# One core, a non-local block and two scans: the last stage in pieces, part of it summed ahead, six places for weighed states, diagonals by ScalarE

## The reference, cut to what matters

```python
attention = theta_x @ phi_x / n                    # theta_x, phi_x, g_x: 1x1 convolutions of x
out = conv1x1((attention @ g_x), w_rec, b_rec) * inv + (bn_beta - bn_mean * inv) + x

def _mamba(u, ...):                                # u: 224 sequences of 56 tokens, 256 features
    x, z = split(u @ in_w.T)                       # 512 and 512
    x = silu(conv_b + sum(xpad[:, k:k + L] * conv_w[:, k] for k in range(4)))
    dt_raw, Bm, Cm = split(x @ xp_w.T)             # 16, 16, 16
    dt = softplus(dt_raw @ dt_w.T + dt_b)
    h = exp(dt * A) * h + (dt * x) * Bm            # a scan over the 56 tokens, 512 x 16 states
    y = (sum over states of h * Cm) + x * D
    return (y * silu(z)) @ out_w.T
out = cat_conv_w @ concat([y1, y2]) + cat_conv_b + x
```

## Time and profile before

| | us |
|---|---|
| median of 3 runs | 5613.23 (5611.07 to 5613.51) |
| the profiled execution's own time | 5617.14 |
| its span, first to last instruction | 5615.2 |

### The profile page before, as it was taken

How to read it: one execution, slowest core, us unless ns; L and a number is a source line. 1 busy time by engine, 2 the same in 40 slices (tenths; PEclk the granted TensorE clock), 3 DMA queues, 4 the chain that set the end, 5 groups by cost and what they waited for, 6 DMA issues and landing times. The chain is left out here.

```text
span 5615.2 us, 71207 instructions
## 1 busy us (share of the span) xinstructions
PE 4836.0 (86%) x26046; PEld 3541.9 (63%) x26046; DVE 5064.4 (90%) x3469; ACT 3547.9 (63%) x5534; POOL 5064.0 (90%) x2582
## 2 busy tenths in 40 slices
PE   8888888888888888888788888889989898888887
PEld 7746566656666565656556656666666666666664
DVE  4469999999999999999999999999999999999992
ACT  0067676766666676767566767666666666766662
POOL 0079999999999999999999999999999999999992
PEclk9989999999999999999899999999999999999999
DMA  4232323232232323232323232333232424242423
GB/s 153 102 109 67 116 67 112 77 102 91 89 108 71 116 67 116 67 112 78 111 67 116 67 112 81 109 104 114 93 125 87 134 80 138 77 144 75 140 70 127
DMA packets 242753, 560.65 MB, mean 100 GB/s; under 512 B 29314, under 2 KB 116226, under 8 KB 241252
## 3 DMA queue, kind: packets, MB, share of 16 engines
q1 hardware_dynamic: 230804, 528.00, 29.2%
q10 hardware_dynamic: 11600, 28.10, 1.3%
HBM read 497.86 MB, written 58.15 MB: 99 GB/s over the span
## 5 line engine op out<-in xcount | busy, mean ns | idle before, releaser
L1058 POOL TENSOR_TENSOR dbx<-dtx,b_all 128x896 f32<-128x896 f32 x1792 | 3701.3, 2102 | 0.1
L986 DVE TENSOR_TENSOR_SCAN mamba_ps<-mamba_ps,dbx 128x896 f32<-128x896 f32 x1232 | 2481.8, 2014 | 106.4 <-ACT mamba_ps L860 63.5
L805 PE MATMUL mamba_ps<-ident,hc 128*112 128x128 f32 x14336 | 1867.5, 282 | 167.0 <-POOL hc L1065 135.9
L805 PEld LDWEIGHTS mamba_ps<-ident,hc 128*112 128x112 f32 x14336 | 1668.7, 138 | 507.4 <-issue 255.3
L860 ACT ACTIVATE mamba_ps<-dt,w 128x448 f32<-128x448 f32 x1792 | 1067.7, 629 | 727.3 <-DVE hc L993 580.8
L993 DVE TENSOR_TENSOR hc<-mamba_ps,c_all 128x896 f32<-128x896 f32 x1232 | 1341.7, 1089 | 137.8 <-DVE mamba_ps L986 3.9
L860 ACT ACTIVATE mamba_ps<-dt,a_next 128x448 f32<-128x448 f32 x1792 | 1067.4, 629 | 626.4 <-DVE hc L993 500.9
L1065 POOL TENSOR_TENSOR hc<-hc,c_all 128x896 f32<-128x896 f32 x560 | 1176.0, 2100 | 130.8 <-DVE hc L986 130.4
L986 DVE TENSOR_TENSOR_SCAN hc<-mamba_ps,dbx 128x896 f32<-128x896 f32 x560 | 1129.1, 2016 | 51.0 <-ACT mamba_ps L860 50.9
L702 PE MATMUL mamba_ps<-u,w 128*128 128x448 f32 x1792 | 799.6, 584 | 203.8 <-ACT sz L883 109.3
L713 PE MATMUL mamba_ps<-x,taps 128*128 128x448 f32 (+3 forms) x1792 | 727.0, 550 | 117.2 <-ACT x L874 108.3
(11 more groups left out here) (107 smaller groups left out, 3105.9 us busy)
## 6 DMA issues: line engine op xcount, KB each, us to landing
b_all<-bc_scratch SPq DMA_DIRECT2D x448, 448.0 KB, 5.5
c_all<-bc_scratch SPq DMA_DIRECT2D x448, 448.0 KB, 4.8
u<-u_scratch SPq DMA_DIRECT2D x56, 448.0 KB, 3.3
y_scratch<-ytok SPq DMA_DIRECT2D x56, 448.0 KB, 3.3
src<-y_scratch SPq DMA_DIRECT2D x80, 224.0 KB, 4.5
u_scratch<-ub ACTq DMA_DIRECT2D x28, 448.0 KB, 4.6
xb<-in_x ACTq DMA_DIRECT2D x3, 3136.0 KB, 10.7
src<-in_x SPq DMA_DIRECT2D x40, 224.0 KB, 5.2
```

The lines of the kernel that those rows point to most:

```text
L805: ins = nc.tensor.matmul(y_ps[j % 2][:, c * 128:(c + 1) * 128], hc[g][:, e * T + c * TCH:e * T + (c + 1) * TCH], ident[:, :], start=False, ...
L986: nc.vector.tensor_tensor_scan(dst, h, dbx[n % BX_RING][:, :], 0.0, ALU.mult, ALU.add).then_inc(scan_done, 1)
L1058: nc.gpsimd.tensor_tensor(view(dbx[n % BX_RING], 0, [[T, 2], [1, T]]), view(dtx, j * T, [[0, 2], [1, T]]), view(b_all, 2 * g * T, [[T, 2], ...
```

## The change

- **Schedule.** All slots of the items are new; fa and fb become one item pair f0, f1 of 448 columns, at TensorE's slot 26 and ScalarE's 26 and 29. Three gates move.
- **Pieces and partial sums.** Tiles 29 to 35 get f0 and f1 too: for batch 3 they sum the first model's two blocks and the map's two (eight matmuls of 448), with the bias, and store that to `part_dram`. Tiles 36 to 55 make the full pieces as before.
- **`finish`.** For batch 3 only the second model's two blocks remain (four matmuls per piece); VectorE adds the stored part, loaded over ScalarE's queue. The last piece of batch 2 is made whole between pieces 4 and 5.
- **Places and lags.** `hc` has six places by `n % 6`; `by_pool` keeps ten slots of 32, but with 27 where 30 was; `POOL_LAG` is 5.
- **Diagonals.** At the change ScalarE makes `taps` and `skip`. The convolution waits for its own four diagonals only.
- **Prologue.** The normalisation's chain is cut into steps, one behind each of the pairs 1 to 13 of batch 0.

```diff
 SCHEDULE = {
-    "z0": (0, 0), "x0": (0, 0), "x1": (0, 2), "z1": (0, 3), "z2": (2, 4), "z3": (2, 5), "c0": (4, 5), "c1": (6, 8),
-    "y3": (7, None), "x2": (9, 10), "x3": (10, 11), "c2": (11, 12), "c3": (12, 13), "y0": (13, None), "out0": (15, 17), "xp": (16, 19),
-    "out1": (18, 20), "dt0": (19, 22), "dt1": (19, 22), "fa0": (21, 23), "dt2": (21, 23), "dt3": (22, 24), "fa1": (23, 26), "y1": (24, None),
-    "y2": (31, None), "fb0": (31, 31), "fb1": (31, 31),
+    "x0": (0, 0), "x1": (0, 0), "z0": (0, 1), "z1": (0, 2), "z2": (1, 4), "c0": (4, 6), "z3": (4, 6), "c1": (6, 8),
+    "y3": (9, None), "x2": (9, 10), "x3": (12, 12), "c2": (12, 12), "c3": (12, 14), "y0": (13, None), "out0": (16, 18), "xp": (17, 18),
+    "out1": (17, 20), "dt0": (19, 21), "dt1": (21, 23), "dt2": (21, 23), "dt3": (23, 23), "y1": (25, None), "f0": (26, 26), "f1": (26, 29),
+    "y2": (31, None),
 }
-TAKE_Y_AT = {5: 3, 13: 0, 22: 1, 28: 2}
-GATE_AT = {8: 3, 15: 0, 25: 1, 29: 2}
+TAKE_Y_AT = {5: 3, 14: 0, 22: 1, 29: 2}
+GATE_AT = {8: 3, 14: 0, 24: 1, 30: 2}
...
-FIN, FIN_FROM = T // 2, TILES + TPB + 1
-FIN_TILES = range(FIN_FROM, 2 * TILES)
+PART_FROM, FIN_FROM = TILES + 1, TILES + TPB + 1
+FIN_TILES = range(PART_FROM, 2 * TILES)
...
-BX_RING, HC_RING = 5, 8
+BX_RING, HC_RING = 5, 6
 def by_pool(n):
-    return n % (2 * GP) in (1, 4, 6, 10, 14)
+    return n % SLOTS in (1, 4, 6, 10, 14, 17, 20, 22, 26, 27)
-POOL_LAG, SUMS_LAG = 3, 4
+POOL_LAG, SUMS_LAG = 5, 4
...
                 def first_half(b):
                     for i in range(PAIRS):
                         take_pair(b, i)
+                        if b == 0 and i >= 1:
+                            next(steps, None)
...
                     for m in range(1 if part else 2):
                         sp.dma_start(s[:, 2 * m:2 * m + 2, :], y_img[m][b][:, :, i * T:(i + 1) * T]).then_inc(src_ready, 16)
...
-                        if g == 2:
-                            between(t - 1)
...
+                    blocks = (0, 1, 4, 5) if part else range(6)
+                    for k in blocks:
-                        ins = nc.tensor.matmul(b[:, 0:FIN], m, src[:, k * FIN:(k + 1) * FIN], start=(k == 0), stop=(k == 5))
+                        ins = nc.tensor.matmul(bank[:, 0:T], m, src[:, k * T:(k + 1) * T], start=(k == 0), stop=(k == 5))
...
+                def make_taps(j):
+                    if j == 0:
+                        act.wait_ge(front_loaded, 32)
+                    act.wait_ge(work_ready, Item(CHANGE - 1, f"c{j}").ready())
+                    for k in range(j * DCONV, (j + 1) * DCONV):
+                        ins = nc.scalar.activation(taps[:, k * 128:(k + 1) * 128], ident[:, :], ACT.Copy, scale=w[:, W_CW + k:W_CW + k + 1])
+                    ins.then_inc(taps_ready, 1)
...
                         decays(SLOTS * t + n)
+                        if t == CHANGE - 1 and n < DB:
+                            make_taps(n)
+                        if t == CHANGE - 1 and n == SLOTS - 1:
+                            make_skip()
...
+            @block.tensor            # of finish
+                for i in range(TPB):
+                    pe.wait_ge(y1_ready[i], 16)
+                    if i >= 3:
+                        pe.wait_ge(taken, i - 2)
+                    for oc in range(2):
+                        for k in range(2):
+                            ins = nc.tensor.matmul(out_bank(i, oc), cat_t[:, (2 + k) * CH + oc * 128:(2 + k) * CH + (oc + 1) * 128],
+                                                   y1[i][:, k * T:(k + 1) * T], start=(k == 0), stop=(k == 1))
+                    ins.then_inc(made, 1)
+                    if i == 4:
+                        pe.wait_ge(whole_ready, 16 * 4)     # then 12 matmuls of the whole piece
+            @block.vector
+                for i in range(TPB):
+                    dve.wait_ge(part_ready[i], 16)
+                    dve.wait_ge(made, i + 1)
+                    for oc in range(2):
+                        h = part[i][:, oc * T:(oc + 1) * T]
+                        ins = nc.vector.tensor_tensor(h, out_bank(i, oc), h, ALU.add)
+                    ins.then_inc(taken, 1)
```

More of the change, by code:

```diff
@@ L476, in _ @@
                     take_turn(n)
[L477 to L498, removed]
                 first_half(0)
@@ L633, in between @@
-                def between(t):
-                    if t in FIN_TILES:
-                        load_src(t, 1)
-                        store_out(t, 0)
+                    to = part_dram[i] if part else out[b].rearrange("(k p) n -> p k n", p=128)[:, :, i * T:(i + 1) * T]
+                    sp.dma_start(to, res[:, :].rearrange("p (k n) -> p k n", k=2)).then_inc(out_stored, 16)
                 def spread_bc(t):
@@ new lines, in _ @@
+                for i in range(TPB):
+                    sp.wait_ge(taken, i + 1)
+                    sp.dma_start(piece(image(out[last]), i), halves(part[i])).then_inc(stored, 16)
+                sp.wait_ge(stored, 16 * TPB)
+            @block.scalar
+            def _(act):
+                for i in range(TPB):
+                    act.dma_start(halves(part[i]), part_dram[i]).then_inc(part_ready[i], 16)
+                    if i == 3:
+                        b, n, _ = left
+                        s = whole[:, :].rearrange("p (k n) -> p k n", k=6)
+                        act.dma_start(now[:, :], k_dram[b]).then_inc(whole_ready, 16)
+                        for m in range(2):
+                            act.dma_start(s[:, 2 * m:2 * m + 2, :], piece(y_img[m][b], n)).then_inc(whole_ready, 16)
+                        act.dma_start(s[:, 4:6, :], piece(image(x_in[b]), n)).then_inc(whole_ready, 16)
+                act.wait_ge(whole_made, 1)
+                for oc in range(2):
+                    ins = nc.scalar.activation(done[:, oc * T:(oc + 1) * T], whole_bank(oc), ACT.Identity, bias=now[:, 2 * CH + oc:2 * CH + oc + 1])
+                ins.then_inc(whole_taken, 1)
+                act.wait_ge(whole_taken, 1)
+                act.dma_start(piece(image(out[b]), n), halves(done)).then_inc(whole_taken, 16)
+                act.wait_ge(whole_taken, 17)
@@ L1117, in _ @@
             @block.tensor
             def _(pe):
-                pe.wait_ge(fixed, 16 + 16 * len(batches))
-                for j, (b, i) in enumerate(jobs):
-                    now = maps[b - b0]
-                    pe.wait_ge(src_ready[j], 48)
-                    if j >= 4:
-                        pe.wait_ge(taken, j - 3)
-                    for oc in range(2):
-                        o = ((j % 4) * 2 + oc) * 512
-                        for k in range(6):
-                            w = cat_t[:, k * CH + oc * 128:k * CH + (oc + 1) * 128] if k < 4 else \
-                                now[:, (k - 4) * CH + oc * 128:(k - 4) * CH + (oc + 1) * 128]
-                            ins = nc.tensor.matmul(ps[:, o:o + T], w, src[j][:, k * T:(k + 1) * T], start=(k == 0), stop=(k == 5))
-                    ins.then_inc(made, 1)
```

184 lines of the change are left out of this document (96 added, 88 removed).

## The result

The changed kernel took 5525.68 us (median of 4 runs, 5521.40 to 5533.96) against 5613.37 for the kernel before (4 runs): a ratio of 0.9845, with an interval of 0.9828 to 0.9862. The forecast was 5481 with a range from 5447 to 5525: the sign was right, the size was not, and the time lies just above the range. The profiled execution took 5525.94 us (span 5524.1), 40.9 more than the 5485 forecast for it.

A forecast was written before the change was run, and what follows sets the result against it. VectorE's own chain was taken to bound the plain tile, GpSimd just under it. Terms -45 - 76.9 + 10.8 + 2 + 2.8 + 0.5 - 21.2 - 5 gave -132 from 5613.2: 5481 us, range 5447 to 5525.

The forecast's parts named there:

- the plain tile's turn: Passage between tiles: TensorE's sum of slot 27, x0 and x1 end late at low clock; +0.4 us a tile, between 0 and 1.6.
- the late tiles' term: Tiles 36 to 54: the stall at scan 0 goes, leaving the plain tile's pace; 1732.8 us for 1809.7, -76.9.
- reload loop: Rival, SyncE's queue: C of pair 3 waits for slot 27's weighing, delaying B of pair 4; +56 us, 5537; chance 0.08.
- Last stage and last tile: End of kernel: 96 matmuls become 40, so the last stage takes 43.6 us for 88.5, -45; last tile +0.5.
- the 1 us for the whole piece's transfers: Last stage: 1 us added for waiting for the whole piece's four transfers, within the 43.6 us.
- Diagonals: Tiles 27 and 28: ScalarE makes the diagonals instead of VectorE; 204.0 us falls to 182.8, -21.2.
- Prologue: Before the tiles: TensorE's 9.08 us wait for VectorE shrinks, the raw transposes then wait for raw_a; -5 us, between -9 and 0.
- TensorE does not bound the late tiles: Rival, late tiles: TensorE's items don't fit, 2.5 us a tile on 20 tiles; +50 us, 5531; chance 0.08.
- Better: Rival, 54 tiles: new slots also remove VectorE's 0.8 us behind table switches, down to GpSimd's floor 90.34; 5438 us; chance 0.08.
- Slower: Rival: six places and later weighing stall each plain turn 4.8 us on 34 tiles, late ones keep theirs; 5708 us; chance 0.04.

## Why the size was off

**The step that failed is the plain tile's turn** (0.4 us a tile between 0 and 1.6), which the late tiles' term took over. It measured 1.0 in plain and late tiles, mostly not for the reason that it priced. The 0.4 stood for TensorE alone, late behind the weighing; the run with C three pairs behind, which leaves that and takes only the loads out of the way, gives 0.2 for it, within its range. What the sum held at nothing is the wait of products 4 and 5 for their loads of B, and that was 0.7 to 0.8 us a tile. The queue behind that wait, SyncE's, I did work through, as the rival *reload loop*, with the right place and the right price (+1.0 a tile, 5537), and gave it 0.08.

**Why it got so little.** I landed B of pair 4 in 5.5 us, the median over all 448 such loads. But the weighing releases a burst, in which the first B takes 5.6 and the second 7.8, so the wait is mostly product 5's (0.95 us a tile, product 4's 0.12, means of tiles 3 to 24), and pair 5 I had not looked at. And I set the weighing's end (85.8) from the cap of five `dbx` places at slot 25, that is from a GpSimd that is never late: right without the loop (86.0), 1.5 us early within it. A need at 91.9 against 91.8 was no margin at all; it should have been read as an even chance.

**Late tiles.** Apart from the loop the step held: 1725 us with the lag of 3 or 4 (forecast 1732.8), and the items' place is the whole gain.

**Last stage and last tile**, 5.9 us short. The stage took 44.9 and not 43.6: TensorE began 1.6 us later than in the sum and was 0.8 us longer over its matmuls, and the 1 us for the whole piece's transfers wasn't needed. The first `y1` landed late since ScalarE's loads ran beside it; held back, it came 3.1 us sooner. The Trainium skill (DMA: Bandwidth & Descriptors, "Issuing engines are not separate DMA queues") says that transfers from several engines run on the same 16 DMA engines and interleave; the 7.46 and 4.3 us of the same load agree. Of the rest 1.1 us is the loop's, in the last tile's own slots. The tail is 3.7 us longer: from the start of the last scan to the last stage's first load 22.6 us for 18.9. There the clock is low for 10.2 us, and the last output projection takes 9.04 us for 7.16. I had no term for it.

```profile
5457.90:5468.10 10.20, 6.78 (x21) 5.10 (x22) 2.46 (x3) 0.59 (x1) 0.00 (x0) 0.50 0.01 2
5464.28 9.04 PE L750 MATMUL mamba_ps<-w,sz 128*112 128x256 f32 x32 [0.72 <-DVE sz L990]
```

What sets the clock there (the rows show it low behind single sums with waits between them) I did not test.

**Diagonals.** -21.2 forecast, -21.6 alone. (The 0.26 us that I gave for one of VectorE's is the row's minimum; its median is 0.28.) ScalarE needs 390 ns for one (I had taken 360). Scans 1 and 2 of tile 27 wait 1.27 and 0.68 us in the changed kernel, but not at all with the diagonals alone or with the lag of 3 or 4, so the four in a slot had room until the loop took it. The Trainium skill's 387 ns (ScalarE: Activation LUTs, "What ACT_TABLE_LOAD costs") was the better figure, and the trace agrees:

```profile
L893 ACT ACTIVATE taps<-ident,w x16: 387/390/399, 2792.7 to 2805.3; 128x128 f32<-128x128 f32 x16
```

**Prologue.** -5 forecast, -3.9 measured, by the mechanism forecast: the wait passed to `raw_a`. That its late landing is itself not fixed (7.0 to 7.7 us in the traces of three kernels that left this load alone, 14.2 to 15.5 in the others) I had not seen, with one trace to go by. Of the 58 us between the changed kernel and the one with a lag of 3 none is the prologue's: their first scans come at 316.2 and 316.5.

**The other rivals.** TensorE does not bound the late tiles (83.54 us busy of 92.00). *Better* did not come: without the loop the plain tile is 90.76 us, and the 0.8 under the old one is not there. *Slower* needs the old schedule beside the new states.

## What to carry to other kernels

When an operation moves later, list every queue that waits for it, and in each in-order queue what stands behind that wait: here a load of C held two loads of B whose own buffers were long free, and letting one B go first gave back 0.8 of the 1.0 us a tile. Price a transfer that a wait releases by the landing of the second and third of the burst, not by the median. A rival that decides by a margin smaller than the error of its own inputs deserves an even chance. Here the sign of the loop was a tile 1 us longer at equal busy time of VectorE and GpSimd.

## What the runs showed of the hardware

A small load can land with a large one that is issued after it: `raw_a` (32 KB a load) left at 20.48, the image at 22.40, and both landed at 35.1 to 35.3 us, whereas with the image held back `raw_a` took 6.7 us. It doesn't always happen: in three traces it landed in 7.0 to 7.7 us beside the same image. Putting another load last only passed this on to it (14.2 us for `raw_dt`). Through the wait and the clock behind it this small load moves the first scan from 306 to 309 us to 316 to 319. Why the two land together no run shows.
